# A pre-norm decoder layer on one core: row means sent ahead of stores and loads, table fills later, seven small steps moved

## The reference

```python
x = x + attn(layernorm(x), queries, combiners)          # linear attention, no softmax
x = x + xattn(layernorm(x), ctx, ctx, Wq, bq, Wk, ...)  # softmax attention over the context
x = x + ffn(layernorm(x), router, 16 experts, shared)   # top 2 of 16 experts, capacity 640 rows each
```

## Time and profile before

| what | us |
|---|---|
| median of 3 runs (1937.49 to 1941.55) | 1941.48 |
| profiled execution, its time | 1936.91 |
| its span in the trace | 1935.2 |
| TensorE busy | 1847.6 (95% of the span) |
| VectorE, ScalarE, GpSimd busy | 831.8, 743.9, 876.7 |
| phase 1, periods from one A to the next from sequence 2 on | about 72 each |
| experts, each | 58.0 |

### The profile page before, as it was taken

The page is one execution under the profiler, slowest core; times in us unless marked ns, Lnnn a source line. Parts: engine busy times, 40 slices in busy tenths (PEclk is TensorE's granted clock), DMA queues, the critical chain, the costliest instruction groups (busy, mean ns, idle before and its releaser), DMA issues.

```text
span 1935.2 us, 27049 instructions
## 1 busy us (share of the span) xinstructions
PE 1847.6 (95%) x10096; PEld 1626.1 (84%) x10096; DVE 831.8 (43%) x2015; ACT 743.9 (38%) x1460; POOL 876.7 (45%) x759
## 2 busy tenths in 40 slices
PE   7798988988989999999999999999999999999997
PEld 4686877876877788788889999999999999999997
DVE  3463663563566444444333432343432333432332
ACT  2243433433446333333244443444443444443431
POOL 2234334334356242322465565665565665565631
PEclk9898999998999999999999999999999999999999
DMA  8112213113126333322276666666666666666632
GB/s 280 30 47 99 81 50 111 69 50 115 44 98 180 44 45 44 76 45 44 52 175 126 147 158 147 142 147 133 147 157 148 144 145 134 145 157 148 143 58 28
DMA packets 218098, 209.68 MB, mean 108 GB/s; under 512 B 137424, under 2 KB 137424, under 8 KB 217712
## 3 DMA queue, kind: packets, MB, share of 16 engines
q1 hardware_dynamic: 192672, 154.85, 30.4%
q0 software_dynamic: 25296, 53.11, 16.3%
HBM read 129.63 MB, written 48.92 MB: 92 GB/s over the span
## 4 chain that ended last, share of the span: by engine, by line
PE 92%; issue 3%; DMA 2%; DVE 1%; SPq 1%; ACT 1%; POOL 0%; ACTq 0%; DVEq 0%; POOLq 0%
PE ps L71 61%; PE ps L1417 22%; PE ps L775 3%; PE ps L911 2%; PE ps L781 1%; PE ps L876 1%; DMA means<-mean 1%; DMA buffer<-means 0%; SPq L262 0%; POOL buffer L374 0%; SPq L271 0%; ACT buffer L1233 0%; DVE buffer L1319 0%; DMA buffer<-in_wts 0%; ACT buffer L1275 0%
## 5 line engine op out<-in xcount | busy, mean ns | idle before, releaser
L71 PE MATMUL ps<-buffer,buffer 128*128 128x320 f32 (+1 forms) x6816 | 1227.6, 341 | 3.5 <-DVE buffer L676 2.1
L71 PEld LDWEIGHTS ps<-buffer,buffer 128*128 128x128 f32 x6816 | 1105.9, 188 | 109.9 <-issue 3.6
L1175 POOL TENSOR_TENSOR buffer<-buffer,buffer 128x512 fp32r<-128x512 f32 x289 | 379.6, 1478 | 246.9 <-ACT buffer L1233 246.4
L1417 PE MATMUL ps<-buffer,buffer 128*128 128x512 f32 x1904 | 437.3, 390 | 0.7 <-DVE buffer L1319 0.6
L1417 PEld LDWEIGHTS ps<-buffer,buffer 128*128 128x128 f32 x1904 | 356.1, 188 | 74.6 <-POOL buffer L1175 1.9
L1233 ACT ACTIVATE buffer<-buffer 128x512 fp32r<-128x512 f32 (+1 forms) x491 | 293.8, 651 | 163.8 <-PE ps L1417 90.9
L1275 ACT ACTIVATE buffer<-ps 128x320 f32<-128x320 f32 (+1 forms) x240 | 112.4, 468 | 589.8 <-PE ps L71 587.9
L1335 DVE TENSOR_TENSOR ps<-ps,buffer 128x320 f32<-128x320 f32 (+2 forms) x198 | 100.1, 506 | 490.5 <-ACT buffer L1275 490.5
L1222 POOL DMA_INDIRECT out_tokens<-buffer,slot_list x80 | 125.9, 1574 | 185.6 <-DVE buffer L1365 180.0
L415 POOL DMA_INDIRECT slots<-pairs,slot_u x64 | 63.5, 992 | 187.3 <-DVE slot_u L762 170.0
L428 ACT ACTIVATE buffer<-buffer,shift,rstd 128x512 f32<-128x512 f32 x96 | 70.4, 805 | 174.6 <-DVE shift L569 174.6
(11 more groups left out here) (114 smaller groups left out, 1128.8 us busy)
## 6 DMA issues: line engine op xcount, KB each, us to landing
buffer<-in_wts SPq DMA_DIRECT2D x289, 256.0 KB, 3.0
buffer<-in_x SPq DMA_DIRECT2D x8, 1024.0 KB, 10.7
buffer<-in_xT SPq DMA_DIRECT2D x8, 1024.0 KB, 5.3
buffer<-in_ctxT SPq DMA_DIRECT2D x8, 1024.0 KB, 8.0
out_tokens<-buffer SPq DMA_DIRECT2D x8, 1024.0 KB, 4.3
tokens_normed<-buffer SPq DMA_DIRECT2D x32, 256.0 KB, 2.5
out_tokens<-buffer POOLq DMA_DIRECT2D x32, 256.0 KB, 6.4
buffer<-means SPq DMA_DIRECT2D x8, 256.0 KB, 5.8
```

The lines of the kernel that those rows point to most:

```text
L71: last = pe.matmul(out, left, right, start=(c == 0 and i == 0), stop=(c == len(parts) - 1 and i == 2))
L1175: pool.tensor_tensor(wl[n % RING][:], wraw[n % RAW][:], wh[n % RING][:].bitcast(F32), ALU.subtract).then_inc(s_wl, 1)
L1417: ins = pe.matmul(down_bank[n % 2][:], left, right, start=(c == 0 and i == 0), stop=(c == FC - 1 and i == len(passes) - 1))
```

## The change

- Step MEAN moves ahead: in SyncE's list it stands right behind LN0 and so ahead of the stores of the sequence two before, which become a step of their own, STORE. STORE(i-1) stands behind MEAN(i+1) in period i. For SyncE the stores and the next load of x thus come behind the wait for the means. GpSimd's part of PV stays where it was.
- At the start, x of sequences 1 and 2 is loaded behind the row of means of sequence 0.
- GpSimd's table fills (padding rows, slot table) run behind MEAN(0) and no longer wait for CT and QT. They take their zeros from a row of their own, and the wait for the padding goes to PV(0).
- The first context is loaded outside the list at the same place in the queue.
- ScalarE's third norm of sequence 7 (step Y2) runs behind the first Silu.
- ScalarE runs a Silu of one number behind the router's Exp.
- LP(0), LX, L1, L2(0), TOK(1), X(0) and the first scatter come one unit (X(0) two) later; X(1) comes behind LP(2).
- One of five weight splits moves from group 3 to group 4.
- In the last group ahead of the experts, the last two tiles of tokens are prepared one down projection earlier.

```diff
-            if name == "C":
-                if b >= 1:
-                    sp.wait_ge(s_cl, NC * b)
-                sp.dma_start(craw[:], a["ctxT"][b].rearrange("(c p) k -> p c k", p=P)).then_inc(s_c, 16)
-                if b == 0:
-                    for first in range(1, XS):
-                        load_x(first)
+            if name == "C" and b >= 1:
+                sp.wait_ge(s_cl, NC * b)
+                load_context(b)
...
                 sp.dma_start(mean_row[:], means[b].partition_broadcast(P)).then_inc(s_mrow, 16)
+                if b == 0:
+                    for first in range(1, XS):
+                        load_x(first)
...
-            if name == "PV":
+            if name == "STORE":
                 rows = slice(b * S, (b + 1) * S)
...
-        pool.wait_ge(s_w, 32)
...
-        pool.wait_ge(s_pad, 32)
...
+        pool.memset(zeros[:], 0.0).then_inc(s_zero, 1)
+        def fill_tables():
...
                     pool.tensor_tensor(xT[:, c, :], xT[:, c, :], mean_row[:], ALU.subtract).then_inc(s_centred, 1)
+                if b == 0:
+                    fill_tables()
...
             if name == "PV":
+                if b == 0:
+                    pool.wait_ge(s_pad, 32)
...
-            if name == "LN2" and b == B - 1:
+            if name == "Y2" and b == B - 1:
                 normalise_x2(b)
...
+                act.activation(table_probe[:], eps_col[:], ACT.Silu)
...
-        steps = [("Y1T", i), ("V", i), ("ST0", i + 1), ("LN0", i + 1), ("INIT", i + 1), ("Q", i), ("G", i + 1),
-                 ("MEAN", i + 1), ("QB", i + 1), ("T", i + 1), ("WV", i + 1), ("SC", i), ("M", i + 1), ("PT", i),
+        steps = [("Y1T", i), ("V", i), ("ST0", i + 1), ("LN0", i + 1), ("MEAN", i + 1), ("STORE", i - 1),
+                 ("INIT", i + 1), ("Q", i), ("G", i + 1), ("QB", i + 1), ("T", i + 1), ("WV", i + 1), ("SC", i), ("M", i + 1), ("PT", i),
                  ("C", i + 1), ("A", i + 1), ("LN1", i + 1), ("PV", i), ("LN2", i)]
...
-    router = {(0, 0): [("LP", 0)], (0, 1): [("LX", 0), ("L1", 0), ("L2", 0)], (0, 2): [("TOK", 1)], (0, 3): [("X", 0)],
-              (1, 0): [("LP", 1), ("TOK", 2)], (1, 1): [("LX", 1), ("L1", 1), ("L2", 1)], (1, 2): [("X", 1), ("LP", 2)],
+    router = {(0, 1): [("LP", 0)], (0, 2): [("LX", 0), ("L1", 0), ("L2", 0)], (0, 3): [("TOK", 1)], (0, 5): [("X", 0)],
+              (1, 0): [("LP", 1), ("TOK", 2)], (1, 1): [("LX", 1), ("L1", 1), ("L2", 1)], (1, 2): [("LP", 2), ("X", 1)],
...
+    RING_REST = [(3, 0), (3, 1), (3, 2), (3, 3), (4, 0)]
...
-        if g == 3 and step in range(RING - WC):
-            return [WC + step]
+        if (g, step) in RING_REST:
+            return [WC + RING_REST.index((g, step))]
...
-        for t in range(max(tiles_of[g], after)):
-            if t < after:
-                yield "x", g + 1, t
-            if t < tiles_of[g]:
-                yield "down", g, t
+        surplus = max(after - tiles_of[g], 0)
+        for t in range(tiles_of[g]):
+            for x in [t] if t < tiles_of[g] - 2 or not surplus else range(t + (t > tiles_of[g] - 2), t + 1 + surplus):
+                if x < after:
+                    yield "x", g + 1, x
+            yield "down", g, t
...
+                    if u == 0:
+                        step("Y2", B - 1)
```

More of the change, by code:

```diff
@@ L167, in phase1 @@
     eps_col = sb("eps_col", [P, 1], F32)
+    table_probe = sb("table_probe", [P, 1], F32)
     x = [at(row, [NT, D]) for row in (46, 92, 18)]
@@ L171, in phase1 @@
     xT = at(8, [NC, S])
-    mean_row = at(42, [S])
+    mean_row, zeros = at(42, [S]), at(43, [D])
     G = at(12, [H * P])
@@ L287, in sync, with load_context @@
         load_transposed(0)
+        def load_context(b):
+            sp.dma_start(craw[:], a["ctxT"][b].rearrange("(c p) k -> p c k", p=P)).then_inc(s_c, 16)
+        load_context(0)
         def step(name, b):
-            if name == "C":
-                if b >= 1:
-                    sp.wait_ge(s_cl, NC * b)
-                sp.dma_start(craw[:], a["ctxT"][b].rearrange("(c p) k -> p c k", p=P)).then_inc(s_c, 16)
-                if b == 0:
-                    for first in range(1, XS):
-                        load_x(first)
+            if name == "C" and b >= 1:
+                sp.wait_ge(s_cl, NC * b)
+                load_context(b)
             if name == "MEAN":
@@ L352, in gpsimd @@
             pool.iota(pairs[:, :, k, :, 0].bitcast(I32), [[S, B], [P, NT]], 0, 1).then_inc(s_const, 1)
-        pool.memset(vh[:, 0, :].bitcast(F32), 0.0).then_inc(s_zero, 1)
-        pool.wait_ge(s_zero, 1)
-        pool.wait_ge(s_w, 32)
[L357 to L360, removed]
-        pool.wait_ge(s_pad, 32)
[L363 to L367, removed]
+        pool.memset(zeros[:], 0.0).then_inc(s_zero, 1)
+        def fill_tables():
+            pool.wait_ge(s_zero, 1)
+            for dst, dt in ((Y, U16), (out, F32)):
+                row = zeros[:].bitcast(dt)
+                pool.dma_start(dst[N:N + PAD, :].rearrange("(t p) d -> p t d", p=P),
+                               row.unsqueeze(1).to_broadcast([P, PAD // P, row.shape[1]])).then_inc(s_pad, 16)
+            pool.memset(slot_list[:, :, 1], 0.0).then_inc(s_empty, 1)
+            pool.iota(slot_list[:, :, 0].bitcast(I32), [[0, E], [1, ET]], N, ET).then_inc(s_empty, 1)
+            pool.wait_ge(s_empty, 2)
+            pool.dma_start(slots.rearrange("(e p t) k -> p e (t k)", e=E, t=ET),
+                           slot_list[:].rearrange("p (e t) k -> p e (t k)", e=E)).then_inc(s_fill, 16)
         def step(name, b):
@@ L1009, in phase2 @@
     for i in range(-1, B):
-        steps = [("Y1T", i), ("V", i), ("ST0", i + 1), ("LN0", i + 1), ("INIT", i + 1), ("Q", i), ("G", i + 1),
-                 ("MEAN", i + 1), ("QB", i + 1), ("T", i + 1), ("WV", i + 1), ("SC", i), ("M", i + 1), ("PT", i),
+        steps = [("Y1T", i), ("V", i), ("ST0", i + 1), ("LN0", i + 1), ("MEAN", i + 1), ("STORE", i - 1),
+                 ("INIT", i + 1), ("Q", i), ("G", i + 1), ("QB", i + 1), ("T", i + 1), ("WV", i + 1), ("SC", i), ("M", i + 1), ("PT", i),
                  ("C", i + 1), ("A", i + 1), ("LN1", i + 1), ("PV", i), ("LN2", i)]
         if i == B - 1:
-            steps = [("Y1T", i), ("V", i), ("Q", i), ("SC", i), ("V2", i), ("PT", i), ("V3", i), ("PV", i),
-                     ("LN2", i)]
+            steps = [("Y1T", i), ("STORE", i - 1), ("V", i), ("Q", i), ("SC", i), ("V2", i), ("PT", i), ("V3", i), ("PV", i),
+                     ("LN2", i), ("STORE", i)]
         if i == -1:
@@ L1032, in phase2 @@
                 order.append(("RAW", 0))
-    router = {(0, 0): [("LP", 0)], (0, 1): [("LX", 0), ("L1", 0), ("L2", 0)], (0, 2): [("TOK", 1)], (0, 3): [("X", 0)],
-              (1, 0): [("LP", 1), ("TOK", 2)], (1, 1): [("LX", 1), ("L1", 1), ("L2", 1)], (1, 2): [("X", 1), ("LP", 2)],
+    router = {(0, 1): [("LP", 0)], (0, 2): [("LX", 0), ("L1", 0), ("L2", 0)], (0, 3): [("TOK", 1)], (0, 5): [("X", 0)],
+              (1, 0): [("LP", 1), ("TOK", 2)], (1, 1): [("LX", 1), ("L1", 1), ("L2", 1)], (1, 2): [("LP", 2), ("X", 1)],
               (1, 3): [("LX", 2), ("L1", 2), ("L2", 2)], (1, 5): [("X", 2)]}
-    scatter_after = {(0, 4): 0, (1, 3): 1, (1, 5): 2}
+    scatter_after = {(0, 5): 0, (1, 3): 1, (1, 5): 2}
     for b in range(3, B):
```

## The result

| what | before | after |
|---|---|---|
| median, us | 1941.51 (4 runs, 1937.49 to 1942.8) | 1866.2 (4 runs, 1865.53 to 1869.18) |
| profiled execution, us | 1936.91 | 1865.53 |
| its span, us | 1935.2 | 1863.8 |

The ratio is 0.9618, 95% interval 0.9601 to 0.9636: 3.8% faster, 2.2 us above the forecast of 1864. The span is 71.4 us shorter: TensorE is idle for 60.3 us less (87.6 before, 27.3 after) and busy for 11.1 us less.

The account below looks back on a forecast made before the run. TensorE's work plus some 87 us idle bounds the kernel. Terms 48.8 + 11.3 + 10.1 + 0.7 + 3.9 = 74.8 off 1936.9 give 1862.1, plus 1.9: 1864 us; forecast 1857 to 1870, range 1856 to 1880.

Parts of the forecast that it names:

- What bounds the kernel: Whole kernel: TensorE's work plus some 87 us idle; the late row of means makes the six waits, 48.8 us.
- The means ahead of the stores, 48.8 us: Sequences 2 to 7: storing the means first removes the six gaps ahead of A; gain 48.8 us, bounds 0 and 48.8.
- X = 18: Sequences 2 to 7: the means may land up to 18 us after issue with the wait still all hidden.
- rival (a): Phase 1: the new wait delays stores and GpSimd; slower kernel if the landing passes 29 us; 2 in 100.
- 302.6 + X: Sequence 3: time in us when GpSimd's subtractions would end if the means land X us after issue.
- The slow A, 11.3 us: A in sequences 2 to 7: the pause lowers TensorE's clock; without gaps 11.3 us come back, bounds 0 and 11.3.
- Rival (c): A in phase 1: slow for another reason, such as GpSimd's subtractions beside it, so the loss stays: 1875; 6 in 100.
- The start, 10.8 us: Start: A(0) at 47.8 instead of 57.94, gain 10.1 us (bounds 0 and 16.6), plus 0.7 for A(0) itself.
- takes 4.92, and MEAN(0) follows with 4.93: Start, GpSimd: C(0) begins at 37.9 and takes 4.92 us, MEAN(0) 4.93, so A(0) comes at 47.8.
- The start of phase 2, 3.9 us: Start of phase 2: waits of 1.9, 0.6 and 1.4 us go; sum 3.9, ends 1 and 5.
- The one-number Silu and the split: Phase 2: no wait with a price in the rows; both taken at 0, ends -1 and +1 us.
- The median: Whole kernel: 1.9 us added to the profiled 1862.1, between the lowest run's 0.6 and the median's 4.6.

Follow-up runs that it names:

- experiment 1: Kernel before with only SyncE's order changed, MEAN ahead of STORE: 1881.96 us against 1948.87, ratio 0.9643.
- Experiments 6 and 7: Changed kernel with the means stored and awaited two or three times in a row: 1927.6 us (ratio 0.9892) with two, 2011.19 (1.0328) with three.
- Experiment 5: Kernel before with 5 to 9 unread matmuls in the gap ahead of each A from sequence 2 on: 1927.74 us against 1937.4.
- experiment 10: Changed kernel with all three subtractions of the start on VectorE (second form): 1856.91 us, ratio 0.9583; the unaltered changed kernel beside it took 1863.63.
- experiment 9: Changed kernel with x of sequences 1 and 2 loaded ahead of the means again: 1863.75 us in one run, changed kernel 1863.63.
- experiment 4: Kernel before with 11 to 18 unread matmuls in the gap ahead of each A from sequence 2 on: 1969.41 us, slower.

## Why the prediction was right

**What bounds the kernel: right.** The order alone took the six gaps away (experiment 1), with the means stored and fetched as worked out.

**The means ahead of the stores, 48.8 us: right in sum, off in one part.** The landing, put at 10 us, took 8.3 to 11.2 in sequences 2 to 7. The copies restarted 7.3 us after the first tile's issue (270.53 to 277.86) and not 3.8. The tile now goes out 0.4 us behind the 1 MB of `out` and no longer 1.1, which may be the reason, but was not tried. So the slack was 4.5 to 6.4 us and not 8, and the bound of the hidden wait, put at X = 18, was measured at 14 to 16. With the landing times that came, neither mattered, but the margin was smaller than the prediction says. Experiments 6 and 7 show that the bound did exist, and the way of rival (a). Its sizes were too mild: by 302.6 + X the kernel with three stores, at X = 31.4, would have been 15 us slower than the kernel before (6 x 5.0 - 14.7), and it was 63. A straight line between the two times measured (20.6 us under the kernel before at X = 20.1, 63 us over it at 31.4), an estimate, puts the break-even at X = 23 and not 29.

**The slow A, 11.3 us: right, and the reason too.** From A(1) to A(7)'s end gaps and slow A together were put at 60.1 and measured 60.0. Experiment 5 shows the cause. The window of A(2) in the changed kernel (columns as in the earlier trace rows):

```profile
168.90:172.50 3.60, 3.60 (x33) 3.58 (x33) 3.60 (x7) 2.89 (x6) 2.12 (x2) 1.00 0.00 0
```

The granted clock is 1.00, the upper of the two levels, where A behind a pause had 0.69. The Trainium skill, page "TensorE: Matmul & The Clock Gate", Part 1, says that throttled is the default and that activity releases it; this case's traces agree, 0.69 behind a pause of 8.5 us and 1.00 without one. Rival (c) is out.

**The start, 10.8 us: mis-sized, 7.5 came.** The direction held, and GpSimd was the last to be ready, as I had taken it. The step that failed is "takes 4.92, and MEAN(0) follows with 4.93". These durations are from stretches in which VectorE did not run its four large subtractions beside GpSimd; moved forward, the eight ran into VectorE's four and took 5.85 and 5.81. C(0) also began at 38.47, not 37.9, which together makes 2.4 us. The trace of the kernel before had a sign of it: beside the same C(0), VectorE took 5.67 us for a subtraction of 64 columns, which took 0.22 us in experiment 10, where GpSimd subtracted nothing.

```profile
42.71 5.67 DVE L616 TENSOR_TENSOR rwp<-rw,rwp 128x64 fp32r<-128x64 f32 x1
```

And A(0) took 6.37 us instead of the 5.4 I took from the mean of the six. This term is not settled by one trace: in a second trace of the same kernel A(0) took 5.17, and A(1) came 2.8 us earlier, at the same start of A(0). The granted clock from 50.3 to 55.6 was 0.50 in the first trace and 0.73 from 50.2 to 55.3 in the second, and only the first has another stretch at 0.50, from 72.7 to 76.1. Held against the one trace of the kernel before, the second gives 10.3 us for the start. So the late start of A(0), 2.4 us, stands in both traces, and what lies behind it is spread by 2.8 us from one to the other. The loads of x ahead of the means did delay the row, by 2.5 us (landed at 41.9 and 39.4, experiment 9), and not by the 7.5 that I had worked out from their bytes; for A(0) they had no weight.

**The start of phase 2, 3.9 us: right,** 4.1 between the two traces (2.9 with the second trace of the changed kernel), by the waits named, 1.9, 1.4 and 0.6 us, which are gone. The one-number Silu and the split were not tried by themselves, so that their 0 is not shown. That the number of table switches stays holds: ScalarE loaded its tables 18 times before and 18 times after.

**The median.** 1.9 us were added to the profile's time; 0.7 it was. The sum of 74.8 stood 3.4 us above the 71.4 that came, nearly all of it at the start. Less the 1.2 us put on too much for the median, this makes the 2.2 by which 1864 was low: the two errors partly cancel, which is luck.

## What to carry to other kernels

A small transfer that others wait for belongs ahead of the large ones in its queue, even where it brings a wait with it, as long as one works out what stands behind that wait: here two row buffers made the stores feed back on GpSimd, and the bound was 14 to 16 us for a wait of 8.3 to 11.2. A short gap in TensorE costs more than its length, since the work behind it runs at a lower clock; here 1.9 us for each. Where GpSimd is the bottleneck of a stretch, look at what VectorE reads beside it before taking a duration from elsewhere, and look for a small VectorE instruction that takes unaccountably long there.

## What the runs showed of the hardware

- Subtractions of two fp32 tensors in SBUF, four of 128x512: 2.50 us on VectorE alone, 4.92 on GpSimd alone, but 5.83 and 5.85 where they overlapped in part, and 6.36 and 6.31 where they overlapped nearly throughout. One subtraction beside the other engine's took 1.75 us on VectorE (0.68 alone) and 1.71 on GpSimd (1.26 alone). Twelve on VectorE alone (7.3 us) were done earlier than eight on GpSimd beside four on VectorE (11.6 us).
- A store of 512 single numbers took 16.1 us to land at the start of the changed kernel, 10.2 in sequence 1, 8.2 to 8.4 in sequences 2 to 4 and 9.9 to 11.1 in 5 to 7; of two or three stores in a row each took some 10 us. Why the later ones take longer was not tried.
- An fp32 matmul of 512 columns from fp32 operands took 0.86 us in a row of such and two instructions, at a granted clock of 1.00 (experiment 4).
- The gaps ahead of A were 48.8 us in the first trace and 52.9 and 55.5 in two kernels with the old order on another chip, where the kernel before took 7 us longer. The changed kernel was not run on that chip; elsewhere it took 1866.2 and 1863.6, where the kernel before took 1941.5 and 1937.4.
